# Retention output from halves, the maxima cut on GpSimd and one bank for a batch's logits, in a perceiver block

## The reference

```
x = x + xattn(layernorm(x), ctx, ctx, mask)          # 16 heads of 16
x = x + retention(layernorm(x))                      # 4 heads, values 128 wide
x = x + ffn(layernorm(x))                            # 8 experts, dense

retention:  o = chunk_retention(rot(q), rot(k), v, gamma)
            o = o * rsqrt(mean(o*o) + eps) * gnorm_w
            o = o * (g * sigmoid(g))
            return o.reshape(B, T, 512) @ Wo.T       # the retention output
ffn:        p = softmax(x @ gate_w + gate_b)         # 8 joint logits per token
            w = p * (p >= 0.1);  w = w / sum(w)
            out = sum_e w[:, e] * (x @ expert_w[e] + expert_b[e])
```

## Time and profile before

| what | value |
|---|---|
| three executions | 207.29, 207.33, 207.42 us |
| median | 207.33 us |
| profiled execution | 208.21 us, of it 206.3 us span |
| granted TensorE clock, mean | 0.995 of full speed |
| instructions in the span | 5923 |
| TensorE busy | 194.6 us |
| VectorE busy | 142.8 us |
| ScalarE busy | 108.0 us |
| GpSimd busy | 70.1 us |

### The profile page before, as it was taken

The page is one execution under the profiler, slowest core; times in us unless marked ns, Lnnn a source line. Parts: engine busy times, 40 slices in busy tenths (PEclk is TensorE's granted clock), DMA queues, the critical chain, the costliest instruction groups (busy, mean ns, idle before and its releaser), DMA issues.

```text
span 206.3 us, 5923 instructions
## 1 busy us (share of the span) xinstructions
PE 194.6 (94%) x2446; PEld 133.2 (65%) x2446; DVE 142.8 (69%) x297; ACT 108.0 (52%) x230; POOL 70.1 (34%) x72
## 2 busy tenths in 40 slices
PE   8998999889999989998999999999999999998991
PEld 8566654446566647565666755477778887877780
DVE  3482578997396484698889636279676486996893
ACT  3235667758586575786979896243416333201200
POOL 8407894355073040068949341001003013010000
PEclk9999999999999999999999999999999999999997
DMA  5979965328119586066000000000000000000001
GB/s 180 289 200 271 322 155 145 99 65 219 45 41 243 114 289 263 3 219 195 5 5 5 3 0 3 0 0 5 0 0 0 3 0 2 3 2 27 25 30 35
DMA packets 15827, 18.10 MB, mean 88 GB/s; under 512 B 2656, under 2 KB 14896, under 8 KB 15792
## 3 DMA queue, kind: packets, MB, share of 16 engines
q1 hardware_dynamic: 14496, 17.30, 28.5%
q10 hardware_dynamic: 1296, 0.34, 0.8%
HBM read 9.81 MB, written 0.52 MB: 50 GB/s over the span
## 4 chain that ended last, share of the span: by engine, by line
PE 73%; DVE 9%; DMA 6%; ACT 3%; SPq 3%; issue 3%; POOL 0%; DVEq 0%; ACTq 0%
PE bank L904 11%; PE bank L981 11%; PE bank L999 11%; PE bank L861 4%; PE bank L847 4%; DVE cneg L1828 4%; PE bank L1199 3%; PE bank L1049 3%; PE bank L1088 3%; DMA ctxT<-in_ctxT 3%; PE bank L1219 3%; PE bank L1092 3%; PE bank L1089 3%; PE bank L1221 2%; PE bank L1220 2%
## 5 line engine op out<-in xcount | busy, mean ns | idle before, releaser
L1828 DVE TENSOR_REDUCE cneg<-bank 128x1 f32<-128x896 f32 x64 | 67.8, 1089 | 24.9 <-PE bank L904 24.9
L1507 ACT ACTIVATE prob<-bank 128x512 f32<-128x512 f32 x112 | 64.3, 600 | 15.9 <-PE bank L981 14.6
L981 PE MATMUL bank<-qstack,kstack 100*32 100x256 bf16 x896 | 43.8, 273 | 1.7 <-ACT prob L1507 1.2
L904 PE MATMUL bank<-kstack,qstack 97*32 97x448 bf16 x512 | 36.9, 354 | 2.6 <-DVE cneg L1828 0.9
L981 PEld LDWEIGHTS bank<-qstack,kstack 100*32 100x32 bf16 x896 | 23.7, 96 | 20.4 <-ACT prob L1507 4.0
L999 PE MATMUL bank<-prob,vals 128*32 128x256 f32 x448 | 34.8, 381 | 0.0
L605 POOL TENSOR_TENSOR nw<-nw,halves 128x2 f32<-128x2 f32 (+1 forms) x10 | 8.2, 825 | 63.5 <-DVE nw L1711 45.2
L904 PEld LDWEIGHTS bank<-kstack,qstack 97*32 97x32 bf16 x512 | 12.4, 95 | 9.9 <-DVE cneg L1828 4.4
L999 PEld LDWEIGHTS bank<-prob,vals 128*32 128x32 f32 x448 | 12.8, 109 | 4.6 <-issue 2.9
L1219 PE MATMUL bank<-exp_high,xn_high 128*128 128x512 f32 (+1 forms) x36 | 14.3, 396 | 0.0
L847 PE MATMUL bank<-ctxT,wk 128*128 128x448 f32 x32 | 13.8, 552 | 0.4 <-DMA ctxT<-in_ctxT 0.4
(11 more groups left out here) (182 smaller groups left out, 320.3 us busy)
## 6 DMA issues: line engine op xcount, KB each, us to landing
kstack<-kpart SPq DMA_DIRECT2D x21, 224.0 KB
w_late<-in_w_ret SPq DMA_DIRECT2D x1, 1536.0 KB, 6.6
mask_all<-in_mask SPq DMA_DIRECT2D x2, 512.0 KB, 4.3
ctxT<-in_w_exp SPq DMA_DIRECT2D x1, 1024.0 KB, 5.3
kpart<-in_w_exp SPq DMA_DIRECT2D x1, 1024.0 KB, 9.1
ctxT<-in_ctxT SPq DMA_DIRECT2D x2, 448.0 KB, 5.0
ctxT<-in_ctxT SPq DMA_DIRECT2D x1, 896.0 KB, 8.1
qstack<-acc SPq DMA_DIRECT2D x12, 64.0 KB, 3.6
```

The lines of the kernel that those rows point to most:

```text
L904: mm = pe.matmul(out[j4:j4 + COLS, :], qstack[0:MROW + 1, h, b, qt * P + j4:qt * P + j4 + COLS], kstack[0:MROW + 1, b, h, half_ * HC:(half ...
L981: mm = pe.matmul(out[j4:j4 + COLS, hh * NQ:(hh + 1) * NQ], kstack[0:KROWS, b, h, kt * P + j4:kt * P + j4 + COLS], qstack[0:KROWS, h, b, :] ...
L1507: act.activation(prob[:, n % PROBS, :], bank[:, c.score_bank(u, jj), :], ACT.Exp).then_inc(c["prob_ready"], 1)
L1828: dve.tensor_reduce(cneg[:, st % 2, i:i + 1], bank[:, pair:pair + 2, 0:HC], AXXY, ALU.max, negate=True).then_inc(c["max_read"], 1)
```

## The change

Three things are changed.

1. **Retention output.** ScalarE writes `y_high` (fp32r, with the factor `gn`) from the turned bank, VectorE `y_low` (`take_low_y`: bank times `gn` minus `y_high`), GpSimd splits `w_reto` into `reto_high` and `reto_low` behind its second late root. `retention_out` is 12 one-pass matmuls of 256 columns for a tile instead of 4 in fp32: 8 with `y_high`, then, once `y_low` is there, 4 with it. It also waits for the split.
2. **Maxima of stages 1 to 6.** GpSimd cuts them (`cut_maxima`, four operations, each behind the one before) as soon as the stage's last tile is reduced. VectorE goes on with the next stage's tiles; its first tile of a stage from 2 on waits until the stage but one before is cut. GpSimd's waits without a need are replaced by these cuts.
3. **Logits.** Both tiles of a batch lie side by side in one side bank (32 columns), with one signal; VectorE takes them with two additions of 16 columns in place of four of 8.

The core of the diff:

```diff
-SIDES = [("ro", 0), ("ro", 1), ("logit", 0), ("logit", 1), ("ro", 2), ("ro", 3), ("bias", 0),
-         ("logit", 2), ("logit", 3), ("bias", 1)]
+SIDES = [("ro", 0), ("ro", 1), ("logit", 0), ("ro", 2), ("ro", 3), ("bias", 0), ("logit", 1), ("bias", 1)]
...
                     root(NB + n, width, first)
+                    if n == 1:
+                        pool.tensor_copy(reto_high[:, :, :], w_reto[:, :, :]).then_inc(s["split"], 1)
+                        pool.wait_ge(s["split"], SPLIT_ALL + 1)
+                        pool.tensor_tensor(reto_low[:, :, :], w_reto[:, :, :], reto_high[:, :, :].bitcast(F32), ALU.subtract).then_inc(s["split"], 1)
+                        pool.wait_ge(s["split"], SPLIT_OUT)
...
+            def cut_maxima(st):
+
+                mp = mpart[:, st % 2, :, :, :]
+                mv = cneg[:, st % 2, :].rearrange("p (t h) -> p t h", t=QT)
+                pool.wait_ge(*only.at("max_read", TILES * (st + 1)))
+                pool.wait_ge(*only.at("max_cut", st))
+                if st >= 2:
+                    pool.wait_ge(*only.at("rows_turned", st - 1))
+                pool.tensor_copy(mp[:, :, 1, :], mv).then_inc(s["cut_chain"], 1)
+                pool.wait_ge(s["cut_chain"], 3 * st - 2)
+                pool.tensor_tensor(mrest[:, :, :], mv, mp[:, :, 1, :], ALU.subtract).then_inc(s["cut_chain"], 1)
+                pool.wait_ge(s["cut_chain"], 3 * st - 1)
+                pool.tensor_copy(mp[:, :, 2, :], mrest[:, :, :]).then_inc(s["cut_chain"], 1)
+                pool.wait_ge(s["cut_chain"], 3 * st)
+                pool.tensor_tensor(mp[:, :, 3, :], mrest[:, :, :], mp[:, :, 2, :], ALU.subtract).then_inc(only["max_cut"], 1)
+
             def between_cuts(i):
 
                 if i < 2:
-                    pool.wait_ge(*only.at("max_cut", 6 + i))
+                    cut_maxima(5 + i)
...
-                pool.wait_ge(*only.at("max_cut", 2))
+                cut_maxima(1)
                 keys_cut(only, 2)
-                pool.wait_ge(*only.at("max_cut", 3))
+                cut_maxima(2)
                 keys_cut(only, 3)
-
-                pool.wait_ge(*only.at("max_cut", 4))
+                cut_maxima(3)
                 stream_and_bias()
+                cut_maxima(4)
...
                 def retention_out(t):
-                    taken("y", t)
+                    pe.wait_ge(s["split"], SPLIT_OUT)
+                    pe.wait_ge(s["high_taken"], HIGH_AT["y", t] + 1)
                     pe.wait_ge(s["rope_read"], TT)
                     out = side("ro", t)
                     for c in range(4):
-                        mm = pe.matmul(out[:, 0:D], yT[:, c, t * P:(t + 1) * P], w_reto[:, c, :], start=(c == 0), stop=(c == 3))
+                        pe.matmul(out[:, 0:D], y_high[:, c, t * P:(t + 1) * P], reto_high[:, c, :], start=(c == 0), stop=False)
+                        pe.matmul(out[:, 0:D], y_high[:, c, t * P:(t + 1) * P], reto_low[:, c, :], start=False, stop=False)
+                    taken("y", t)
+                    for c in range(4):
+                        mm = pe.matmul(out[:, 0:D], y_low[:, t, c, :], reto_high[:, c, :], start=False, stop=(c == 3))
                     mm.then_inc(s["side_ready"], 1)
...
                 dve.wait_ge(*c.at("max_ready", m + 1))
+                if not c.loop and st > 1 and i == 0:
+                    dve.wait_ge(*only.at("max_cut", st - 1))
...
-                last = m
-                if not c.loop and st > 1 and i == 0:
-                    st, last = st - 1, m - 1
-                elif i < TILES - 1 or not c.loop and 0 < st < STAGES - 1:
+                if i < TILES - 1 or not c.loop and 0 < st < STAGES - 1:
                     return
...
+            def take_low_y(t):
+
+                dve.wait_ge(s["high_taken"], HIGH_AT["y", t] + 1)
+                dve.scalar_tensor_tensor(y_low[:, t, :, :], bank[:, turn_bank("y", t), :].rearrange("p (f q) -> p f q", f=4), gn[:, 0:1],
+                                         y_high[:, :, t * P:(t + 1) * P].bitcast(F32), ALU.mult, ALU.subtract).then_inc(s["turn_taken"], 1)
...
                 decay_weights(RH)
+                take_low_y(0)
                 decay_weights(RH + 1)
+                take_low_y(1)
                 second_stream(0, [lambda: decay_weights(RH + 2)])
...
                 gate_weights(0)
+                take_low_y(2)
                 weight_parts(0)
+                take_low_y(3)
                 add_experts(0, range(0, 6))
```

More of the change, by code:

```diff
@@ L137 @@
 SPLIT_ALL = 14
+SPLIT_OUT = 16
+KSTACK_BYTES = NB * NH * CH * 2
 PER = {"k_ready": 8, "k_hi": 4, "k_rest": 4, "k_taken": 4, "k_mid": 4, "k_cut": 4, "v_ready": NVP + 2, "v_evac": NVP + 2,
@@ L1208, in logits @@
                     taken("n3", t)
-                    out = side("logit", t)
+                    b, i = divmod(t, QT)
+                    if i == 0:
+                        side("logit", b)
+                    out = bank[:, SIDE, i * 2 * NE:(i + 1) * 2 * NE]
                     for c in range(KIN):
                         both = gate_parts[:, c, :, :].rearrange("p i e -> p (i e)")
-                        for i, part in enumerate((xn_high, xn_low)):
-                            mm = pe.matmul(out[:, 0:2 * NE], part[:, c, t * P:(t + 1) * P], both, start=(c == i == 0), stop=(c == i == KIN - 1))
-                    mm.then_inc(s["side_ready"], 1)
+                        for h, part in enumerate((xn_high, xn_low)):
+                            mm = pe.matmul(out, part[:, c, t * P:(t + 1) * P], both, start=(c == h == 0), stop=(c == h == KIN - 1), skip_group_check=True)
+                    if i == QT - 1:
+                        mm.then_inc(s["side_ready"], 1)
                 def split_product(out, t, c, experts):
@@ L1577, in take_y @@
                 def take_y(t):
-                    take_turn("y", t, yT[:, :, t * P:(t + 1) * P], bank[:, turn_bank("y", t), :].rearrange("p (f q) -> p f q", f=4), scale=gn[:, 0:1])
+                    assert TURNS[len(takes)] == ("y", t)
+                    act.wait_ge(s["turned"], len(takes) + 1)
+                    act.activation(y_high[:, :, t * P:(t + 1) * P], bank[:, turn_bank("y", t), :].rearrange("p (f q) -> p f q", f=4), ACT.Copy,
+                                   scale=gn[:, 0:1]).then_inc(s["high_taken"], 1)
+                    takes.append(("y", t))
                 def gate_exp(t):
@@ L1827, in take_maximum @@
                 dve.wait_ge(*c.at("max_ready", m + 1))
+                if not c.loop and st > 1 and i == 0:
+                    dve.wait_ge(*only.at("max_cut", st - 1))
                 dve.tensor_reduce(cneg[:, st % 2, i:i + 1], bank[:, pair:pair + 2, 0:HC], AXXY, ALU.max, negate=True).then_inc(c["max_read"], 1)
-                last = m
-                if not c.loop and st > 1 and i == 0:
-                    st, last = st - 1, m - 1
-                elif i < TILES - 1 or not c.loop and 0 < st < STAGES - 1:
+                if i < TILES - 1 or not c.loop and 0 < st < STAGES - 1:
                     return
-                dve.wait_ge(*c.at("max_read", last + 1))
+                dve.wait_ge(*c.at("max_read", m + 1))
+                if not c.loop and st:
+                    dve.wait_ge(*only.at("max_cut", st))
                 new_maximum(c, st)
@@ L2031, in gate_logits @@
                 def gate_logits(b):
-                    tiles = range(QT * b, QT * b + QT)
                     both = slice(QT * b, QT * b + QT)
-                    for t in tiles:
-                        n_ = SIDE_AT["logit", t] + 1
-                        dve.wait_ge(s["side_ready"], n_)
-                        post(dve.tensor_tensor(glog[:, t, :], bank[:, SIDE, 0:NE], gb_row[:, :], ALU.add))
-                        dve.tensor_tensor(glog[:, t, :], bank[:, SIDE, NE:2 * NE], glog[:, t, :], ALU.add).then_inc(s["side_taken"], 1)
+                    n_ = SIDE_AT["logit", b] + 1
+                    parts = bank[:, SIDE, 0:QT * 2 * NE].rearrange("p (t i e) -> p t i e", t=QT, i=2)
+                    dve.wait_ge(s["side_ready"], n_)
+                    post(dve.tensor_tensor(glog[:, both, :], parts[:, :, 0, :], gb_row[:, :].unsqueeze(1).to_broadcast([P, QT, NE]), ALU.add))
+                    dve.tensor_tensor(glog[:, both, :], parts[:, :, 1, :], glog[:, both, :], ALU.add).then_inc(s["side_taken"], 1)
                     dve.wait_ge(s["side_taken"], n_)
```

13 lines of the change are left out of this document (8 added, 5 removed).

## The result

The changed kernel takes 210.33 us (median; 208.32 to 210.60), the kernel before 207.31 (206.93 to 207.42): ratio 1.0125, interval 1.0075 to 1.0176. It is slower; the forecast was 206.5 us and the range ended at 207.9. The profiled execution took 210.32 us with a span of 208.5, against 208.21 and 206.3. A ratio, with its 95% interval, is estimated without the few executions in the slow state, and can differ a little from the quotient of the two medians.

A forecast was written before the change was run, and what follows sets the result against it. TensorE's waits were taken to bound the kernel. Cuts −0.35, first retention output −0.5, weight split 0 and second batch 0 sum to −0.85 us, from 207.33 to 206.5 us; range 205.9 to 207.9.

The forecast's parts named there:

- What bounds the kernel: Whole kernel: TensorE, busy 194.6 of 206.3 us, so what counts is when TensorE waits.
- the cuts: Attention stages: a maxima cut off VectorE spares TensorE some 0.2 us, mostly lost to the DMA wait; −0.35 us together.
- its own terms, 0.27 and 0.1: Cuts: 0.09 us for each of three stage starts, 0.27; and 0.1 at the start at 75.45 us.
- the term's bound of −1.0: Cuts: the faster end, if five cuts keep their 0.2 us whole.
- The first retention output: First batch, from 161.38 us: 24 one-pass matmuls take 2.87 us instead of 3.45; −0.5 us, bounds 0.4 to 0.6.
- The split of the weights: GpSimd from about 141.2 us, beside VectorE's rope: costs nothing on GpSimd; taken as 0, bounds 0 and +1.2 us.
- slow halves: Retention output, both batches: rival that 24 matmuls take 4.6 us, 1.1 longer in each batch; 209.2 us, chance 0.03.
- The rival on the slower side: Rope, L1969 and L1972: VectorE waits for GpSimd's subtraction, up to +1.2 us; 207.7 or 208.0 us, chance 0.35.
- The second batch: Second batch: VectorE's low halves delay the biases 0.6 us, joint logits recover it; 0, between −0.1 and +0.6 us.

The follow-up runs named there:

- both profiles: Profiles of the changed kernel's first run (210.33 us) and of its unchanged repeat, 209.97 us against 207.10 for the kernel before.
- behind `xn`: Changed kernel, but GpSimd's split of `w_reto` waits only for the `xn` operations: 209.23 us, ratio 1.0079 to the kernel before.
- early: Changed kernel, but the split stands ahead of the second late root and waits for the attention's end: 207.76 us, ratio 1.0030 to the kernel before.
- the split in the gap: Changed kernel, but GpSimd's split of `w_reto` waits for the third tile's rope: 206.11 us against 207.25 for the kernel before, ratio 0.9955.

## Why the prediction was wrong

- **What bounds the kernel, and the cuts: right in mechanism.** TensorE waited as described, the second wait went, the wait for the DMA grew. At the start at 61 us TensorE's gain was 0.30 at the second wait and 0.09 behind the DMA, where 0.2 and 0.09 were forecast (its starts differ from before by 0.74, 0.44 and 0.65 us in turn). At the start at 75 us it was 0.43 (a difference of 0.66 became 0.23), where the prediction took 0.1 and at most 0.4. So the size of −0.35 (its own terms, 0.27 and 0.1, add up to 0.37) is probably too small: 0.2 to 1.3 by the executions, 0.6 to 0.9 by the profiles, inside the term's bound of −1.0. GpSimd's chain took 1.01 us (66.79 to 67.80), forecast 1.04.
- **The first retention output: right.** 0.50 us, forecast 0.5.
- **The split of the weights: the step that failed.** It said "On GpSimd it costs nothing", then looked for VectorE's operations with two SBUF inputs, found L1969 and L1972, set bounds of 0 and +1.2, and took 0. Three things were wrong in it. The operation that was held first is L1714, which the same root releases as the cast behind it, and so met the cast in both profiles; it has one SBUF tile as input and wasn't counted. The hold lasts as long as the GpSimd operation, and there are two holds in a row, 2.83 us instead of 1.2. And TensorE's clock wasn't in the bounds: the stall of 2.2 us cost another 1.4 in the first profile, where the clock fell, as it did by the mean clocks in probably seven of ten executions. "GpSimd releases VectorE only where a row says so" was no reason: no row of before had such a pair beside each other, so the rows could say neither. None of the prediction's rivals reached the measured time; the highest, slow halves, stood at 209.2 us.
- **The rival on the slower side** had the mechanism and the sign; its place was the rope, and not the `xn` ahead of it, and its price less than half. With the split where that rival places it (behind `xn`) the rope's L2015 was held for 1.9 us, as the rival had it, too.
- **The Trainium skill.** SBUF — State Buffer, "Who interferes with whom", states what the runs showed: the two-input rule by the runs behind `xn` and early, and the full block by these and the changed kernel. The same section also says that copy, cast and `tensor_scalar` can enter modes that use both port pairs and then contend; L1714 is a `tensor_scalar`, and the prediction had taken only the sentence on two inputs. The trace agrees with the block, with 1.10 and 2.54 us for what took 0.37; no run here shows in which mode L1714 runs.
- **The second batch: right in sum** (−0.04 us between the first retention output's end and the last logits' maximum), with the biases 0.52 us later than before, where 0.6 was forecast, and the logits level again.

So of 3.0 us slower, the terms that the prediction had right give about −0.9 (the split in the gap, ratio 0.9955), and the split's place +4.2 or +2.8, with or without the clock.

## What to carry to other kernels

Before moving work to GpSimd, list what VectorE runs in that very stretch: here operations that read only SBUF, with one tile or two, were held until a GpSimd cast or subtraction had ended, while those with an input from a bank ran on. Work that is hidden on its own engine isn't hidden when it sits behind the same release as critical work; a wait that puts it into a stretch of bank-fed VectorE work cost nothing here and was worth some 4 us (210.33 and 209.97 to 206.11). And compare two profiled executions with the medians before believing a gain in a stretch that the change hardly touches: here 1.6 of 2.4 us were an accident.

## What the runs showed of the hardware

- Each VectorE operation with SBUF inputs alone that began while a GpSimd cast or subtraction ran was held until within 0.3 us behind its end: 0.37 to 1.10 and 2.54, 0.42 to 2.36 and 2.48, and 0.18 to 0.50 us. The GpSimd operation kept its length (2.38 us for the subtraction, beside a held operation or none). One small row says that the reading matters: a VectorE operation of one column with two SBUF inputs keeps 0.16 us amid a GpSimd memset of 1.80 us, which only writes (17.65 to 17.81 in the kernel before, the memset from 17.26 to 19.06).
- VectorE operations with one input from a bank beside the same GpSimd operations keep theirs: 0.69 us beside the cast, 0.69 and 0.51 beside the subtraction.
- The same stall of TensorE, 2.18 us with 0.5 us of waiting shortly before, cost the clock in one profiled execution (0.50 for some 3 us) and not in another (1.00 from 138 to 152 us), and the kernel's times spread from 208.3 to 211.3.
- A gap of TensorE near 96 us, without a releaser, is absent in some executions and 0.25 to 1.07 us long in others. Its cause stays open.
